# Keeping the output weights of a mixture of experts in TensorE, and weighting the hidden activations instead of the outputs

## What is computed

```
w = softmax(mean(x, 0) @ Wr + br)             # 8 expert weights per row
h = relu(bn1(einsum('bfd,edh->bfeh', x, W1) + b1))
h = relu(bn2(einsum('bfeh,ehk->bfek', h, W2) + b2))
y = einsum('bfeh,ehd->bfed', h, Wo) + bo
return einsum('bfed,fe->bfd', y, w)           # all experts run on every row
```

## Time and profile before

| | us |
|---|---|
| median of 3 runs | 1095.93 (1095.89 to 1095.94) |
| profiled execution, its own time | 1095.72 |
| its span in the profile | 1093.9 |
| TensorE busy | 1082.8 (99%) |
| VectorE busy | 768.1 (70%) |
| ScalarE busy | 732.0 (67%) |
| GpSimd busy | 248.3 (23%) |

### The profile page before, as it was taken

The page is one execution under the profiler, slowest core; times in us unless marked ns, Lnnn a source line. Parts: engine busy times, 40 slices in busy tenths (PEclk is TensorE's granted clock), DMA queues, the critical chain, the costliest instruction groups (busy, mean ns, idle before and its releaser), DMA issues.

```text
span 1093.9 us, 19080 instructions
## 1 busy us (share of the span) xinstructions
PE 1082.8 (99%) x6512; PEld 967.6 (88%) x6512; DVE 768.1 (70%) x1804; ACT 732.0 (67%) x1275; POOL 248.3 (23%) x290
## 2 busy tenths in 40 slices
PE   9999998999999999999999999999999999999998
PEld 7988987988888888888898888888888988889998
DVE  8888756886686676766766767767767667676665
ACT  5777756676675666756756767667567566576665
POOL 4787763312012012030120120210301202100000
PEclk9999999999999999999999999999999999999999
DMA  6878852111011101110110111101101101100000
GB/s 182 270 226 252 243 171 54 60 34 55 1 49 50 40 18 42 40 58 2 44 55 1 49 50 39 47 13 40 59 1 49 50 10 35 35 20 1 1 20 15
DMA packets 71300, 67.91 MB, mean 62 GB/s; under 512 B 20641, under 2 KB 66579, under 8 KB 71203
## 3 DMA queue, kind: packets, MB, share of 16 engines
q1 hardware_dynamic: 66552, 59.34, 18.1%
q0 software_dynamic: 3968, 6.71, 2.4%
q10 hardware_dynamic: 683, 0.64, 0.2%
HBM read 40.87 MB, written 25.80 MB: 61 GB/s over the span
## 4 chain that ended last, share of the span: by engine, by line
PE 91%; POOL 3%; DVE 2%; issue 2%; ACT 1%; DVEq 0%; POOLq 0%; ACTq 0%
PE bank L280 29%; PE bank L281 29%; PE bank L282 29%; PE bank L989 1%; POOL gathered L601 1%; PE bank L1156 1%; PE bank L1164 1%; PE bank L930 1%; PE bank L1179 1%; PE bank L922 1%; POOL gathered L619 0%; POOL alpha_l L621 0%; PE bank L946 0%; DVE sum_squares L1336 0%; DVE activated L1260 0%
## 5 line engine op out<-in xcount | busy, mean ns | idle before, releaser
L1380 DVE SCALAR_TENSOR_TENSOR accumulated<-bank,router_w,accumulated 128x256 f32<-128x256 f32 (+2 forms) x392 | 170.4, 480 | 177.9 <-PE bank L282 171.0
L665 ACT ACTIVATE h<-weight_stage 128x512 fp32r<-128x512 f32 (+2 forms) x206 | 113.6, 599 | 183.9 <-PE bank L282 164.4
L282 PE MATMUL bank<-ffn_w_high,h 128*128 128x256 f32 (+2 forms) x778 | 220.0, 283 | 0.0
L281 PE MATMUL bank<-ffn_w_low,h 128*128 128x256 f32 (+2 forms) x778 | 219.8, 283 | 0.0
L280 PE MATMUL bank<-ffn_w_high,h 128*128 128x256 f32 (+2 forms) x778 | 219.6, 282 | 0.0
L1230 DVE TENSOR_TENSOR h_low<-activated,h_high 128x512 fp32r<-128x512 f32 (+2 forms) x208 | 135.3, 658 | 76.0 <-ACT h_high L665 73.0
L816 ACT ACTIVATE activated<-bank,bn_cols 128x512 f32<-128x512 f32 (+2 forms) x208 | 155.8, 749 | 46.1 <-PE bank L282 44.1
L816 ACT ACTIVATE weight_stage<-bank,bn_cols 128x512 f32<-128x512 f32 (+2 forms) x208 | 152.7, 748 | 41.4 <-PE bank L282 41.0
L280 PE MATMUL bank<-xT_high,ffn_w_high 128*128 128x512 f32 (+2 forms) x416 | 158.9, 382 | 0.1
L280 PE MATMUL bank<-h_high,ffn_w_high 128*128 128x512 f32 (+2 forms) x416 | 157.9, 380 | 0.1
L281 PE MATMUL bank<-xT_low,ffn_w_high 128*128 128x512 f32 (+2 forms) x416 | 157.8, 379 | 0.0
(11 more groups left out here) (228 smaller groups left out, 1917.1 us busy)
## 6 DMA issues: line engine op xcount, KB each, us to landing
x_rows<-in_x SPq DMA_DIRECT2D x18, 512.0 KB, 4.8
x_turned<-xT_high SPq DMA_DIRECT2D x22, 256.0 KB, 3.6
x_turned<-xT_low SPq DMA_DIRECT2D x22, 256.0 KB, 4.7
out<-accumulated SPq DMA_DIRECT2D x11, 512.0 KB, 3.3
mix_xT_high<-x_turned SPq DMA_DIRECT2D x10, 512.0 KB
mix_xT_low<-x_turned SPq DMA_DIRECT2D x10, 512.0 KB
weight_stage<-in_L_ffn_W SPq DMA_DIRECT2D x16, 256.0 KB, 3.2
node_table<-gathered SPq DMA_DIRECT2D x22, 132.0 KB, 2.9
```

The lines of the kernel that those rows point to most:

```text
L281: nc.tensor.matmul(dst, ah, bl, start=False, stop=False)
L282: last = nc.tensor.matmul(dst, al, bh, start=False, stop=(k == n - 1))
L665: return nc.scalar.activation(dst, src, ACT.Copy)
L1380: last = V.scalar_tensor_tensor(a, y_of(ch, e)[b][0:tp, (t % 2) * D:(t % 2 + 1) * D], wts(ch)[0:tp, t, e:e + 1], a, ALU.mult, ALU.add)
```

## The change

For chunk 0 all stays as it was, except that its accumulators lie in one bank and one buffer. For every later chunk:

- L3 holds the output weights in the array and streams h2, 512 columns at a time: twelve matmuls per expert in the form of L2, 2 halves of the output columns by six. All experts add up in the same two PSUM banks (first only clears at expert 0), with output columns on partitions.
- The router weight is applied to the hidden activations: VectorE multiplies the second relu's result by the row's weight (weigh_hidden) before ScalarE rounds it. For this each expert's weights must lie spread over all 128 partitions along the free axis. VectorE transposes them in 32x32 blocks (wblk), SP stores them to DRAM (w_d, four small stores) and loads each expert's 512 weights back with a partition broadcast (wbc, eight loads of 256 KB per chunk, in buffers that are partly borrowed).
- The bias is one matmul per half, with the bias rows held in the array and the high and low weight columns (wT, loaded from w_d) streaming, added into the same banks in iteration 2. router_turn, the ScalarE copy and add_bias fall away.
- After the last expert VectorE transposes each bank in 32x32 blocks out of PSUM (turn_back). x2 goes to DRAM (x2_d) when computed and comes back in the same block form, in 32-number pieces; GpSimd adds the two (final_add; VectorE for the last chunk), and SP stores the sum in 128-byte pieces (eight stores per chunk; in the last chunk sixteen, half of them on ScalarE's queue).
- Only two bias row groups are built at the start. The scratch memory for GpSimd's descriptors is set to 8192 bytes.

```diff
-        bo3 = sb("bo_rows", [P, TPC, D], f32r)
+        bo3 = sb("bo_rows", [P, 2, D], f32r)
+        wT = sb("expert_weight_cols", [3 * NE, CH], f32r)
+        wbc = [wbs[:, 0, :], wbs[:, 1, :], wbs[:, 2, :], wbs[:, 3, :], xb0[:, 0, :], xb0[:, 1, :], tmp[:, 2, :], wst[:, 2, :]]
...
-        def mm3(dst, lhs, rhs, ready=None):
+        def mm3(dst, lhs, rhs, ready=None, first=True, final=True):
...
 SP, per chunk:
+                    load_weights(ch, range(NE - 1, NE))
                     store(ch.prev())
+                    load_x2(ch)
                 if ch.c + 2 < NC:
                     load_rows(CHUNKS[ch.c + 2])
                     load_idx(CHUNKS[ch.c + 2])
                     load_turned(CHUNKS[ch.c + 2])
+                if not ch.last:
+                    store_x2(ch.next())
+                    store_weights(ch.next())
+                    load_weights(ch.next(), range(2))
+                    load_weight_cols(ch.next())
+                    load_weights(ch.next(), range(2, NE - 1))
...
+            def store_weights(ch):
+                need(sp, s["wblk"], ch.c)
+                for a in range(P // Q):
+                    r = min(Q, ch.tp - a * Q)
+                    sp.dma_start(w_d[ch.c, :, 0:ch.rows].rearrange("q (t p) -> q t p", p=ch.tp)[:, :, a * Q:a * Q + r],
+                                 wblk[a * Q:(a + 1) * Q, 0:ch.nt * Q].rearrange("q (t r) -> q t r", r=Q)[:, :, 0:r]).then_inc(s["wds"], 16)
+            def load_weights(ch, experts):
+                need(sp, s["wds"], 16 * (P // Q) * ch.c)
...
+                for e in experts:
+                    if ch.c > 1:
+                        need(sp, s["hw"], weighted(ch.prev(), e))
+                    sp.dma_start(wbc[e][:, 0:ch.rows], w_d[ch.c, 3 * NE + e, 0:ch.rows].partition_broadcast(P)).then_inc(s_wb[e], 16)
+            def load_x2(ch):
+                need(sp, s["x2s"], 16 * ch.c)
+                need(sp, s_out[ch.prev().par], stored_out(ch.prev()))
+                for h in range(2):
+                    for a in range(P // Q):
+                        for mine, theirs in block_parts(ch, h, a, x2_d):
+                            sp.dma_start(mine, theirs).then_inc(s["x2l"], 16)
...
 GpSimd, per chunk:
+                if ch.c >= 3:
+                    final_add(CHUNKS[ch.c - 2])
...
 ScalarE, high2:
+                if ch.c > 0:
+                    need(act, s["hw"], weighted(ch, e, h))
...
 TensorE:
+            def L3(ch, e):
+                if ch.c == 0:
+                    return L3_rows(ch, e)
...
+                for h in range(2):
+                    if e == 0:
+                        if ch.c == 1:
+                            need(pe, s["acc"], NE)
+                        else:
+                            need(pe, s["yt"], 2 * (ch.c - 2) + h + 1)
+                    mm3(Yb[h][:, 0:R], [W(2, e, k, h * P, (h + 1) * P) for k in range(KT)],
+                        [(hi[:, k, 0:R], lo[:, k, 0:R]) for k in range(KT)], hidden if h == 0 else None,
+                        first=(e == 0), final=(e == NE - 1)).then_inc(s["y"], 1)
...
+                need(pe, s["wtl"], 16 * ch.c)
+                for h in range(2):
+                    nc.tensor.matmul(Yb[h][:, 0:ch.rows], bo3[0:3 * NE, 0, h * P:(h + 1) * P], wT[:, 0:ch.rows],
+                                     start=False, stop=False).then_inc(s["fbo"], 1)
...
-                    if e == 0 and ch.c > 0:
-                        router_turn(ch)
...
+                    if e == 2 and ch.c > 0:
                         out_bias(ch)
...
 VectorE:
+            def weigh_hidden(ch, e):
+                R = ch.rows
+                need(dve, s_wb[e], 16 * ch.c)
+                for h in range(2):
+                    need(dve, s["r2"], 2 * NE * ch.c + 2 * e + h + 1)
+                    V.tensor_tensor(act2[:, h, 0:R], act2[:, h, 0:R], wbc[e][:, 0:R], ALU.mult).then_inc(s["hw"], 1)
+            def turn_back(ch):
...
+                need(dve, s["fin"], 2 * (ch.c - 1))
+                for h in range(2):
+                    need(dve, s["y"], y_done(ch, NE - 1, h))
+                    V.transpose(yblk[:, h, 0:w], Yb[h][:, 0:w]).then_inc(s["yt"], 1)
...
 VectorE, in iteration e:
-                    if e > 0:
-                        accumulate(ch, e - 1)
-                    elif ch.c > 0:
-                        accumulate(ch.prev(), NE - 1)
                     if nxt is not None and e == NE - 1:
                         weights(nxt)
-                    if not (ch.last and e == NE - 1):
-                        hid2(ch, e)
-                    if e == 0 and ch.c > 0:
-                        add_bias(ch)
+                    if ch.c == 0:
...
+                    else:
...
+                        weigh_hidden(ch, e)
+                    hid2(ch, e)
+                    if ch.c > 1 and e == 0:
+                        turn_back(ch.prev())
                     if nxt is not None:
                         for step in (FRONT_1 if nxt.c == 1 else FRONT).get(e, ()):
                             step(nxt)
...
-    nc = _bacc.Bacc("TRN2", target_bir_lowering=False, num_devices=1)
+    nc = _bacc.Bacc("TRN2", target_bir_lowering=False, num_devices=1, dynamic_dma_scratch_size=8192)
```

More of the change, by code:

```diff
@@ L219, in build @@
         s_out = [s["out0"], s["out1"]]
+        s_wb = [s[f"wb{e}"] for e in range(NE)]
         s_idx = [s["idx0"], s["idx1"]]
@@ L279, in mm3 @@
                     ready(k)
-                nc.tensor.matmul(dst, ah, bh, start=(k == 0), stop=False)
+                nc.tensor.matmul(dst, ah, bh, start=(first and k == 0), stop=False)
                 nc.tensor.matmul(dst, ah, bl, start=False, stop=False)
-                last = nc.tensor.matmul(dst, al, bh, start=False, stop=(k == n - 1))
+                last = nc.tensor.matmul(dst, al, bh, start=False, stop=(final and k == n - 1))
             return last
@@ new lines, in store @@
+            def store(ch):
+                if ch.c == 0:
+                    need(sp, s["acc"], NE)
+                    sp.dma_start(ch.rows_of(out), acc[0:ch.tp, 0, 0:ch.nt, :]).then_inc(s_out[0], 16)
+                    return
+                for h in range(2):
+                    need(sp, s["fin"], 2 * (ch.c - 1) + h + 1)
+                    for a in range(P // Q):
+                        if ch.last and a >= 2:
+                            continue
+                        for mine, theirs in block_parts(ch, h, a, out):
+                            sp.dma_start(theirs, mine).then_inc(s_out[ch.par], 16)
@@ L481, in _ @@
                     load_turned(CHUNKS[ch.c + 2])
-            store_last(LAST)
-            for par in range(2):
-                need(sp, s_out[par], 16 * sum(ch.nb if ch.last else 1 for ch in CHUNKS if ch.par == par))
+                if not ch.last:
[4 more added lines that the diff above has]
+                    load_weights(ch.next(), range(2, NE - 1))
+            store(LAST)
+            for ch in CHUNKS[-2:]:
+                need(sp, s_out[ch.par], stored_out(ch))
         @block.gpsimd
@@ L547, in bo_rows @@
             def bo_rows():
-                for t in range(TPC):
+                for t in range(2):
                     pch.step(nc.gpsimd.tensor_copy(bo3[t * Q:(t + 1) * Q, t, :], bo_low[t * Q:(t + 1) * Q, :]))
-                for t in range(TPC):
+                for t in range(2):
                     half = slice(t * Q, t * Q + 2 * NE)
@@ L659, in _ @@
                     gather(ch.next(), range(2, ch.next().nt))
+            final_add(LAST.prev())
         @block.scalar
@@ L783, in base_shift @@
                 tp = ch.tp
-                need(act, s_xB[ch.par], 16 * (ch.half + 1))
+                need(act, s_xB[min(ch.c, 1)], 16 * max(ch.c, 1))
                 need(act, s["rsl"], 6)
@@ L914, in _ @@
                         FRONT[e](nxt)
+            for h in range(2):
+                act.wait_ge(s["fin"], 2 * (LAST.c - 1) + h + 1)
+                for a in range(2, P // Q):
+                    for mine, theirs in block_parts(LAST, h, a, out):
+                        act.dma_start(theirs, mine).then_inc(s_out[LAST.par], 16)
         @block.tensor
```

196 lines of the change are left out of this document (122 added, 74 removed).

## The result

| | before | after |
|---|---|---|
| median in the comparison, us | 1095.93 (1095.89 to 1097.4, 4 runs) | 1084.22 (1082.99 to 1084.77, 4 runs) |
| profiled execution, its own time | 1095.72 | 1082.99 |
| its span in the profile | 1093.9 | 1081.2 |

The account below looks back on a forecast made before the run. The prediction took TensorE's instruction stream as the bound. Its terms, -15.2 - 1.4 - 1.2 + 3.1 + 0.3 = -14.4 us, took 1095.93 to 1081.5, stated as 1081, range 1077 to 1092.

Parts of the forecast that it names:

- L3 and the echo: Full chunks: 512-wide L3 saves 0.15 us per expert, the block behind it 0.03; -15.2 us over 11 chunks.
- the width gives nothing: Rival on L3: 512 columns in one piece no cheaper than in two; 1096 us, no change; chance 0.06.
- The router transposes: Transpose of the router weights leaves TensorE for chunks 1 to 12: 0.12 us each, -1.4 us.
- The bias: Bias matmuls stay two 512-wide ones and move into iteration 2: no cost or gain.
- The last chunk's L3: L3 in the last chunk, 378 columns in three tiles: counted at nothing, at most 1.4 us gain.
- The start: First stage: GpSimd builds fewer bias rows, 1.8 us less, so TensorE loses its 1.26 us gap; -1.2 us.
- The end: After the last matmul: a transpose, an addition and more stores, 6.9 us where it was about 3.8; +3.1 us.
- The last expert's multiplications: Kernel end: the last expert's multiplications on VectorE stand open to TensorE; +0.3 us.
- The hand-over: Between chunks: router weights return through DRAM in time for expert 0's L3, slack 1.2 us, no stall counted.
- the rival: Weights come back late at the hand-over: L3 1.7 us late twelve times, 1101 us; chance 0.14 slower, 0.09 smaller stall.
- SP's queue: SP's stores and loads in small pieces, 7.9 us per group; indices landed by 631, nothing late.
- the rival of small packets: SP's queue: 128-byte pieces cost twice, 16 us per group, indices at about 642; 1086 to 1091 us; chance 0.08.

Follow-up runs that it names:

- split run: Against the changed kernel, each L3 matmul of chunks 1 to 12 streams its columns in two pieces: 1103.3 us, ratio 1.0071 to the kernel before.
- the repeat: The changed kernel run once more with no edit: 1084.08 us, ratio 0.989 to the kernel before.
- late run: Against the changed kernel, spread weights of experts 0 and 1 load after those of 2 to 6: 1136.78 us, ratio 1.0359 to the kernel before.

## Why the prediction was right, and where it missed

- **L3 and the echo, -15.2:** right. The blocks are 2.72 as taken, and with the bias at 128 rows a full chunk is 1.47 shorter (74.72 to 73.25), which is the 1.38 + 0.12 of the sum within 0.03. The split run shows that it is the width, with the number of matmuls that goes with it. The rival "the width gives nothing" falls. The prediction also weighed a formula of the Trainium skill ("TensorE: Matmul & The Clock Gate", Back-to-back issue gap), which the skill gives for an isolated matmul. By it, as an estimate, splitting L3 would have cost 3 us in all; it cost 19 (14.9 in full chunks), so the runs do not agree with it here.
- **The router transposes, -1.4:** consistent with the 1.47 and with the 74.98 of the split run, not tested alone.
- **The bias, nothing:** this is the term that failed. "The bias matmuls are two 512-wide ones before and after, and move into iteration 2: nothing" looked at the columns alone. They now have 24 rows in the array, between matmuls of 128, and cost 0.38 more per chunk: +4.6. The diff says bo3[0:3 * NE, ...] and wT is [3 * NE, CH]; I read both and priced only the width. The trace of the kernel before would have warned of it: its 64-row bias matmul in chunk 0 has the same 0.4 around it. That the forecast came within 3.2 us is partly luck: with this cost the sum would have been 1086.1, and other terms came out some 3 us cheaper than it had them.
- **The last chunk's L3:** counted at nothing, with up to 1.4 as the bound. One of its L3 blocks takes 2.08 where it took 2.14 (1083.70 behind 1081.56 in the kernel before), so eight of them gained 0.5. (The 0.6 that the trace gains behind 1006.81 also hold the last three L3 blocks of the chunk before, a bias pair and its cost.)
- **The start, -1.2:** GpSimd's share is right; undoing it costs 1.3. Up to the x2 transposes for chunk 1 this profile gained 2.4, and that of the repeat 0.44 less. Of the 1.2 beyond GpSimd's share a part is thus spread; the rest was not traced to a cause.
- **The end, +3.1:** +1.9. From the last matmul's end (1075.60) to the end of the last issue (1079.44) it takes 3.8 where I had 4.3, and from there to the end of the span 1.8 where I took 2.6.
- **The last expert's multiplications, +0.3:** 0.1. TensorE's last wait on the low part is 1073.48 to 1073.78, 0.30 where 0.17 is usual.
- **Together:** +4.6 for the bias, -0.5 for the last chunk, -1.2 at the start, -1.2 at the end and -0.2 for the multiplications make +1.5 on the sum of -14.4; measured is +1.7.
- **The hand-over, no stall:** right, with 2.5 us of slack where I reckoned 1.2. The round trip is 2 us quicker. The late run shows that the rival was real as a mechanism: 5.3 us of delay minus 2.5 of slack gives the stall. Its price was too low by more than a third, since a stall of 2.7 us cost 4.3 with the slow clock behind it. Its time was also off as written: the 604.8 lets only the load take 6.5 us, and stores of 6.5 in place of 3.7 would have put it at 607.6.
- **SP's queue:** right in that nothing is late, for a wrong size: a group takes 5.7 us and not 7.9, so the rival of small packets, which needed 16, was far off. The 31 ns were a mean over packets of very different size, and what sets the 5.7 is the issuing. The rival had a slip too: two groups longer by 7.9 us each move the indices from 631 to 647, not to 642. The Trainium skill ("DMA: Bandwidth & Descriptors", Specifications) says that transfers under 512 B are done by reading, modifying and writing. Here the 128-byte stores cost 12 ns a packet and the loads 13, so the runs show no surcharge of stores over loads.
- **VectorE's block transpose of 512 columns:** 696 ns against the 0.69 taken, with 1.24 as the other bound.

## What to carry to other kernels

A matmul's price in a dense stream has three parts to look up: its columns, what stands before it, and its number of array rows. Here a pair with 24 rows between matmuls of 128 cost 0.38 us more than the same pair padded with zeros, one matmul with 64 rows cost the same, and a pair with 96 cost nothing; look at where the weight load starts. Where TensorE is the bound, see whether a product can stream 512 columns per matmul, and measure the distance of starts, not busy time. The round trip through DRAM was free here since it had 2.5 us of slack; price a late one with the clock that it costs behind the stall.

## What the runs showed of the hardware that I had not expected

**VectorE and GpSimd slow each other.** The new additions on GpSimd meet VectorE's operations with two arrays in SBUF. Groups by form of the kernel after (busy us, mean ns, then idle before and its releaser):

```profile
L749 POOL TENSOR_TENSOR accumulated<-accumulated,normalised 128x512 f32<-128x512 f32 x22 | 37.8, 1741 | 402.5 <-DVE normalised L1520 402.5
...
L1549 DVE TENSOR_TENSOR residual<-x_rows,b_rows 128x1024 f32<-128x1024 f32 x11 | 20.4, 1857 | 1.3 <-ACT x_rows L903 1.3
...
L1557 DVE TENSOR_TENSOR graph_logits<-gathered,alpha_l 128x16 f32<-128x16 f32 x11 | 11.7, 1063 | 2.5 <-DMA alpha_l<-node_table,indices 2.5
```

VectorE's same two groups in the kernel before:

```profile
L1399 DVE TENSOR_TENSOR residual<-x_rows,b_rows 128x1024 f32<-128x1024 f32 x11 | 13.5, 1225 | 0.0
...
L1407 DVE TENSOR_TENSOR graph_logits<-gathered,alpha_l 128x16 f32<-128x16 f32 x11 | 1.9, 169 | 2.5 <-DMA alpha_l<-node_table,indices 2.5
```

GpSimd's addition takes 1741 ns on the mean (1284 to 2282) where the same form takes 1288 in the first stage, VectorE's 1024-column addition 1857 where it took 1225, and an operation of 16 columns, caught behind, 1063 where it took 169. GpSimd's two additions run from 595.82 to 599.34, and in that time VectorE's 1024-column one starts at 596.18. It costs TensorE nothing here, since VectorE has idle time. That a shared port is the cause was not tested by a run. The Trainium skill ("GPSIMD Engine Reference", 1. Specifications) says that GpSimd's SBUF interfaces are shared with VectorE and contended by VectorE instructions with two SBUF inputs. The rows agree with its direction: 1741 for 1288, 1857 for 1225.

**A stall costs the clock too.** In the late run TensorE was idle for 2.46 us and, 1 us after it had started again, ran at the lower level from 629.45 to 632.83, 1.6 us lost on top of the stall.

**Short packets cost less each, and more per byte.** A packet of 128 bytes takes 12 to 13 ns and one of 1 KB some 59, a fifth of the time for an eighth of the bytes.

**24 and 64 rows in the array stop the weight loads from running ahead, 96 do not.** The loads around the 24-row pair start 0.3 us late, at 64 rows in the kernel before likewise, and at 96 rows, or 128 with zeros, they do not.
